# Query projection made directly in transposed form, with its token scale sent through DRAM, and a head order in the stacked tensors that keeps each transfer's destination in one piece

## The chip, the cores and the metric

The kernel runs on one core of one Trainium2 chip. The time is the device time of one execution in microseconds (us), and of several executions the median is given. TensorE (PE) does the matrix products, VectorE (DVE), ScalarE (ACT) and GpSimd (POOL) the elementwise work, and the sync engine (SP) issues nearly all DMA transfers of the part that the change touches.

## What is computed

A block with cross-attention and a mixture of experts. There are 32 batches of 112 tokens with 512 channels, 16 heads of 32 channels, and a context of 375 rows for each batch. The query projection is quantized: tokens and weight rows are rounded to integers with one scale each.

```python
def _w8a8_linear(x, w, b):
    qx, sx = _dyn_quant(x)            # integers, one scale a token
    qw, sw = _quant_weight(w)         # integers, one scale an output channel
    y = jnp.einsum('bnc,oc->bno', qx, qw) * (sx * sw[:, 0])
    return y + b
...
q = _w8a8_linear(x, wq, bq).reshape(B, N, H, D).transpose(0, 2, 1, 3)
k = (cond @ wk.T + bk).reshape(B, L, H, D).transpose(0, 2, 1, 3)
v = (cond @ wv.T + bv).reshape(B, L, H, D).transpose(0, 2, 1, 3)
scores = jnp.einsum('bhnd,bhld->bhnl', q, k) * inv_sqrt_d + mask[:, None]
attn = jax.nn.softmax(scores, axis=-1)
o = jnp.einsum('bhnl,bhld->bhnd', attn, v)
...
x = x + _L0_xattn_ref(_layernorm(x, axis=-1), ctx_2048, ...)
x = x + _L0_ffn_ref(_layernorm(x, axis=-1), ...)     # top 2 of 8 experts
```

## The kernel before

The program has four parts in a row: `prepare_weights` (to about 35 us of the trace), `attention` (to about 1115 us), `route` (to about 1160 us) and `experts` (the rest). Each part gives every engine a program of its own, and engines meet only at semaphores: `need(engine, semaphore, count)` lets an engine wait. Each engine takes its own instructions strictly in the order written.

`attention` is a software pipeline with one batch an iteration. Iteration `it` does the attention of batch `it` (stage a), the projections of batch n = it+1, the layer norm and rounding of the tokens of batch nn = it+2, the output projection of batch m = it-1 and the second layer norm and router of m2 = it-2. Inside an iteration all engines step through the heads h = 0 to 15. For each head PE turns the probabilities of two heads ago (line 563), makes the scores of head h (line 555), runs a share of the 28 projection steps (lines 591 and 596), and after certain heads a small piece of the other stages. The loop body covers two iterations and is passed 13 times; the first and the last iterations are written out.

The scores use a split of each float into two parts. For a head, the left operand `q_stack` holds 96 rows (q_hi, q_hi, q_lo of 32 channels each) and the right one `k_stack` holds k_hi, k_lo, k_hi. A projection comes out with 128 channels, that is 4 heads, on the partitions and groups of 4 heads side by side, so the stacked tensors are made by 36 small transfers from on-chip memory to on-chip memory in each iteration: 24 for keys (lines 276 to 280, 12 for each half of the heads) and 12 for queries (lines 313 to 317). Transfer i takes partitions 32 i to 32 i + 31, which hold the heads i, i+4, i+8, i+12. In `k_stack` and `q_stack` the heads stand in their natural order, so a destination is written in pieces four heads apart.

The query of batch n runs through these steps:
- h = 6: PE turns the rounded tokens `x_int` into `misc` (line 603), DVE copies them to `x_int_t` (494).
- h = 7: PE multiplies by `wq_int`, tokens on the partitions, four products of 512 columns (638).
- h = 8: DVE scales by the token's scale and by the row of weight scales into `q_tok` (498), POOL adds the bias row (357).
- h = 9: PE turns `q_tok` back, four transposes (603), and ACT makes `q_hi` from the result (424).
- h = 10: DVE makes `q_lo` (502). SP issues the 12 query transfers when it comes to them.

SP's order in one iteration is: 12 transfers of the second half of the keys of batch it, two weight loads (292, 293), the mask load (296), the stores of batch m2 (299, 301), the load of `x_res` (304), 12 transfers of the first half of the keys of batch n, 12 of its queries, the context and token loads (321, 323), and four weight stores (327, 328). The two key groups wait for the scores that still read the old keys (line 277's callers wait on `scored`). POOL's order is: the residual sum and the two small steps of the second norm, the sign of the mask (354), the query bias (357), the bias of `x_res` (361), the first norm's steps, the low part of the context (370) and of a piece of expert weights (375).

Of the kernel before, what the change touches and what calls it, by code (L numbers as in the profile page):

```python
# [4 lines left out]
F32 = mybir.dt.float32  # L5
# [3 lines left out]
ALU = mybir.AluOpType  # L9
# [3 lines left out]
H = 16  # L13
# [5 lines left out]
QUARTER = 32  # L19


def prepare_weights(nc, W, x, ctx_t, wq, wk_t, wv_t, wo, bq, bk, bv, bo, router_t):
# [6 lines left out]
    with ExitStack() as ctx:  # L29
# [10 lines left out]
        spread = sb("w_spread", [128, 2, KT, N])  # L40
# [9 lines left out]
        pairs = (("q", W["wq_int"], W["wq_row"]), ("o", W["wo_int"], W["wo_row"]))  # L50
# [5 lines left out]
        def _(sp):  # L56
# [5 lines left out]
            for dst, src in ((W["bq_row"], bq), (W["bv_row"], bv), (W["bo_row"], bo)):  # L62
                sp.dma_start(dst[:, :], src.rearrange("(a n) -> a n", a=1).to_broadcast([128, C])).then_inc(rows_loaded, 16)
            with nc.allow_non_contiguous_dma(reason="512 biases, once"):
                sp.dma_start(W["bk_col"][:, :], bk.rearrange("(g p) -> p g", p=128)).then_inc(rows_loaded, 16)
# [24 lines left out]
        def _(act):  # L90
# [15 lines left out]
            for i, (_, _, row) in enumerate(pairs):  # L106
                act.wait_ge(row_made, i + 1)
                act.activation(row[0:N, :], ps[0:N, :], ACT.Copy, scale=-inv_sqrt_d if i == 0 else 1.0).then_inc(row_out, 1)

        @block.vector  # L110
        def _(dve):
            for i, (n, _, _) in enumerate(pairs):
# [17 lines left out]
            for i, (_, dst, _) in enumerate(pairs):  # L130
# [6 lines left out]
            dve.tensor_scalar(W["bq_row"][:, :], W["bq_row"][:, :], -inv_sqrt_d, None, ALU.mult).then_inc(bias_done, 1)  # L137

        @block.tensor
        def _(pe):  # L140
            pe.wait_ge(ident_cast, 1)
            for i in range(2):
# [9 lines left out]
                pe.wait_ge(spread_done, KT * (i + 1))  # L152
                if i:
                    pe.wait_ge(row_out, i)
                for t in range(KT):
                    mm = pe.matmul(ps[0:N, 128 * t:128 * t + 128], spread[:, i, t, :], W["ident"][:, :],
                                   start=True, stop=True)
                mm.then_inc(row_made, 1)


def attention(nc, W, x, ctx_t, mask, x1, h2):
# [19 lines left out]
    with ExitStack() as ctx:  # L181
# [22 lines left out]
        q_tok = sb("q_tok", [N, C])  # L204
# [22 lines left out]
        q_made, q_out = sem("q_made"), sem("q_out")  # L227
        q_biased, q_hi_made, q_stacked = sem("q_biased"), sem("q_hi_made"), sem("q_stacked")
# [438 lines left out]
E = 8  # L667
# [512 lines left out]
```

## Time and profile before

| | |
|---|---|
| median of 3 runs | 1607.35 us (1606.39 to 1612.29) |
| profiled execution | 1609.71 us, its span from the first to the last instruction 1608.0 us |
| granted clock of TensorE, mean | 0.965 |
| busy: PE, DVE, ACT, POOL | 1494.6, 897.5, 884.0, 660.6 us |
| `attention` | about 35.8 to 1115 us |

A view of busy time tells how long each engine had an instruction under way. A timeline row gives start, duration, engine, line, operation and tiles. Matrix products overlap, so for PE the distance between two starts is the time that counts, and not the duration of one. "SPq" rows are SP's issue of a DMA: the duration is SP's own time, not the transfer's. What stands in brackets is idle time of the engine before the instruction, and what ended it.

### The profile page before, as it was taken

How to read it: one execution, taken by the hardware profiler on the slowest of the kernel's cores; microseconds unless marked ns; L12 is line 12 of the kernel's file. 1: busy time of each engine (PE TensorE's matmuls, PEld its weight loads, DVE VectorE, ACT ScalarE, POOL GpSimd, SP SyncE). 2: the span in 40 equal slices, each digit the busy share in tenths (PEclk: the TensorE clock that was granted, in tenths of full speed). 3: DMA queues.
4: the chain of work that ended last, by engine and by line, in shares of the span. 5: the costliest groups of instructions: out<-in, count | busy, mean ns of one | idle time of the engine just before them, and what ended most of it. 6: DMA issues, size and time to landing. Idle time of an engine off the chain costs nothing. (4 is left out here: it accounts for less than half of the span.)

```text
span 1608.0 us, 40123 instructions
## 1 busy us (share of the span) xinstructions
PE 1494.6 (93%) x11594; PEld 1317.6 (82%) x11595; DVE 897.5 (56%) x2365; ACT 884.0 (55%) x2097; POOL 660.6 (41%) x671
## 2 busy tenths in 40 slices
PE   2899999999999999999999999984399999999896
PEld 2788888888888888888888888873299999999895
DVE  6557666766676667666766676654632222222221
ACT  2467667677777776777677767761033333333232
POOL 4233334333443234323432343323555555656453
PEclk9999999999999999999999999985599999999998
DMA  5567777677767776777677767654537776666643
GB/s 173 145 170 196 209 200 197 179 228 205 194 178 226 202 196 179 225 205 196 178 225 201 200 179 222 185 142 141 160 68 186 182 175 134 148 154 125 160 77 48
DMA packets 220124, 281.09 MB, mean 175 GB/s; under 512 B 83568, under 2 KB 164976, under 8 KB 220080
## 3 DMA queue, kind: packets, MB, share of 16 engines
q1 hardware_dynamic: 203952, 247.24, 54.3%
q0 software_dynamic: 16128, 33.30, 11.6%
q8 instruction: 23, 0.38, 0.1%
q14 instruction: 21, 0.17, 0.0%
HBM read 118.31 MB, written 66.17 MB: 115 GB/s over the span
## 5 line engine op out<-in xcount | busy, mean ns | idle before, releaser
L464 DVE CUSTOM_DVE_ANT_0 probs<-score,neg_mask 112x375 f32<-112x375 f32 x512 | 279.7, 546 | 254.8 <-PE score L555 251.5
L392 ACT ACTIVATE probs<-probs,neg_max 112x375 f32<-112x375 f32 x512 | 312.3, 610 | 197.2 <-DVE neg_max L464 191.7
L563 PE MATMUL turn<-ident,probs 112*125 112x112 f32 x1536 | 264.8, 282 | 2.8 <-ACT probs L392 2.5
L385 ACT ACTIVATE probs_t<-turn 125x336 f32<-125x336 f32 x512 | 226.0, 441 | 71.6 <-PE turn L563 70.6
L563 PEld LDWEIGHTS turn<-ident,probs 112*125 112x125 f32 x1536 | 227.2, 190 | 36.4 <-issue 14.4
L555 PE MATMUL score<-k_stack,q_stack 96*112 96x376 f32 x512 | 209.4, 409 | 8.5 <-DMA q_stack<-q_lo 6.2
L591 PE MATMUL proj<-ctx_hi,wk_hi 128*128 128x376 f32 x512 | 176.0, 344 | 1.9 <-PEq L29 1.1
L591 PE MATMUL proj<-ctx_lo,wk_hi 128*128 128x376 f32 x512 | 172.0, 336 | 0.0
L591 PE MATMUL proj<-ctx_hi,wk_lo 128*128 128x376 f32 x512 | 171.7, 335 | 0.0
L1032 DVE TENSOR_TENSOR a_lo<-a_ps,a_hi 128x384 fp32r<-128x384 f32 x63 | 35.1, 557 | 243.7 <-ACT a_hi L1007 243.7
L596 PE MATMUL proj<-wv_hi,ctx_hi 128*125 128x512 f32 x384 | 151.8, 395 | 0.0
L596 PE MATMUL proj<-wv_hi,ctx_lo 128*125 128x512 f32 x384 | 151.7, 395 | 0.0
L596 PE MATMUL proj<-wv_lo,ctx_hi 128*125 128x512 f32 x384 | 151.0, 393 | 0.0
L354 POOL TENSOR_SCALAR neg_mask<-neg_mask 112x375 f32<-112x375 f32 x32 | 16.8, 525 | 305.2 <-DMA neg_mask<-mask 305.2
L370 POOL TENSOR_TENSOR ctx_lo<-ctx_stage,ctx_hi 128x1504 fp32r<-128x1504 f32 x31 | 106.6, 3437 | 57.9 <-ACT ctx_hi L429 57.9
L990 POOL DMA_INDIRECT out<-y_rows,scatter_idx x63 | 101.9, 1618 | 57.3 <-POOL scatter_idx L986 50.7
L375 POOL TENSOR_TENSOR w_raw<-w_raw,w_hi 128x1056 fp32r<-128x1056 f32 x32 | 78.9, 2467 | 92.9 <-ACT w_hi L434 92.9
L591 PEld LDWEIGHTS proj<-ctx_hi,wk_hi 128*128 128x128 f32 x512 | 97.4, 190 | 8.7 <-issue 1.5
L1020 ACT ACTIVATE y_rows<-y_ps,row_share 128x512 f32<-128x512 f32 x63 | 43.5, 691 | 106.7 <-PE y_ps L1102 73.3
L555 PEld LDWEIGHTS score<-k_stack,q_stack 96*112 96x112 f32 x512 | 92.4, 181 | 9.9 <-issue 7.5
L591 PEld LDWEIGHTS proj<-ctx_lo,wk_hi 128*128 128x128 f32 x512 | 97.6, 191 | 0.0
L591 PEld LDWEIGHTS proj<-ctx_hi,wk_lo 128*128 128x128 f32 x512 | 96.9, 189 | 0.0
(198 smaller groups left out, 3393.9 us busy)
## 6 DMA issues: line engine op xcount, KB each, us to landing
k_stack<-k_hi SPq DMA_DIRECT2D x512, 94.0 KB, 2.2
k_stack<-k_lo SPq DMA_DIRECT2D x256, 94.0 KB, 2.2
ctx_stage<-ctx_t SPq DMA_DIRECT2D x32, 750.0 KB, 5.0
q_stack<-q_hi SPq DMA_DIRECT2D x256, 56.0 KB, 2.0
w_raw<-gate_up_t SPq DMA_DIRECT2D x32, 352.0 KB, 3.1
gate_up_dram_hi<-w_hi SPq DMA_DIRECT2D x32, 352.0 KB, 4.8
gate_up_dram_lo<-w_raw SPq DMA_DIRECT2D x32, 352.0 KB, 5.2
gate_up_hi<-gate_up_dram_hi SPq DMA_DIRECT2D x16, 704.0 KB, 4.9
```

The source lines that it names most:

```text
L370: pool.tensor_tensor(c_lo[:, par % 2, :, :], stage[:, :, :], c_hi[:, par % 2, :, :].bitcast(F32), ALU.subtract).then_inc(c_lo_made, 1)
L375: pool.tensor_tensor(w_lo[:, :], w_raw[:, :], w_hi[:, :].bitcast(F32), ALU.subtract).then_inc(w_lo_made, 1)
L385: act.activation(probs_t[:, h % RING_T, :, :], turn[h % 2][0:LC, 0:LT * N].rearrange("p (l n) -> p l n", l=LT), ACT.Copy).then_inc(turned_ ...
L392: act.activation(probs[:, h % DS, :], probs[:, h % DS, :], ACT.Exp, bias=neg_max[:, par % 2, h:h + 1], scale=-1.0, accum_out=total[:, par ...
L464: dve.tensor_tensor_reduce(probs[:, h % DS, :], score[h % 2][0:N, 0:L], neg_mask[:, p, :], 1.0, BIG, ALU.add, ALU.min, neg_max[:, p, h:h + ...
L555: pe.matmul(score[h % 2][0:N, 0:LP], q_st[:, par % 2, h, :], k_st[:, h, :], start=True, stop=True).then_inc(scored, 1)
L563: mm = pe.transpose(turn[h % 2][0:LC, l * N:(l + 1) * N], probs[:, h % DS, l * LC:(l + 1) * LC], W["ident"][0:N, 0:N])
L591: mm = pe.matmul(bank[:, 0:LP], W[w][:, t, 128 * u:128 * u + 128], c[:, q, t, :], start=(t == 0 and w == "wk_hi" and c is c_hi), stop=(t = ...
L596: mm = pe.matmul(bank[0:LC, :], c[:, q, t, l * LC:(l + 1) * LC], W[w][:, t, :], start=(t == 0 and w == "wv_hi" and c is c_hi), stop=(t == ...
L990: pool.indirect_dma_start(out, bass.IndirectOffsetOnAxis(ap=si[par][:, 0:1], axis=0), y[:, par, :], None, compute_op=ALU.add).then_inc(sca ...
L1020: act.activation(y[:, other, :], y_ps[other][:, 0:C], ACT.Copy, scale=share[:, other:other + 1]).then_inc(y_made, 1)
L1032: dve.tensor_tensor(a_lo[:, :], a_ps[:, 0:FP], a_hi[:, :].bitcast(F32), ALU.subtract).then_inc(a_lo_made, 1)
```

## The change

The query projection is computed with output channels on the partitions, which is the layout that `q_hi` and `q_lo` need. PE uses `wq_int` as the left operand in 16 products of 128 channels by 112 tokens. The four transposes at h = 9 and their wait for POOL go. The weight scale and the bias then lie along the partitions (`wq_col`, `bq_col`), and the token scale lies along the free axis. `x_scale` is one number a partition, so it is stored to a small DRAM tensor `x_scales` by a new DMA at the end of SP's iteration it for batch nn, and read back one iteration later, repeated to all 128 partitions, by a second new DMA behind the store of `h_rows`. POOL multiplies it by `wq_col` into `q_scale` before the query bias. DVE scales `misc` by `q_scale` into `q_t` at h = 8, POOL adds the bias, ACT makes `q_hi` from `q_t` as soon as the bias is in, and DVE makes `q_lo` from `q_t`.

In `k_stack` and `q_stack` head h now stands at place h % 4 * 4 + h // 4. The heads that one transfer moves are then neighbours. PE picks the place by `stacked_at`.

In `prepare_weights` the row form of the query's weight scale is no longer made (4 products, 4 ACT copies and one eviction fewer). DVE executes 14 semaphore increments ahead of its first iteration (`LOOP_OFFSET`), which no one waits for.

```diff
@@ prepare_weights
-            for i in range(2):
-                act.wait_ge(scale_done, i + 1)
-                for t in range(KT):
-                    act.activation(spread[:, i, t, :], ones[:, :], ACT.Copy, scale=scale[:, i, t:t + 1]).then_inc(spread_done, 1)
+            act.wait_ge(scale_done, 2)
+            for t in range(KT):
+                act.activation(spread[:, t, :], ones[:, :], ACT.Copy, scale=scale[:, 1, t:t + 1]).then_inc(spread_done, 1)
...
+            dve.tensor_scalar(W["wq_col"][:, :], scale[:, 0, :], -inv_sqrt_d, None, ALU.mult).then_inc(bias_done, 1)
@@ attention, SP
-                        sp.dma_start(k_st[QUARTER * r:QUARTER * r + QUARTER, 8 * half + i:8 * half + 8:4, :].bitcast(F32),
+                        sp.dma_start(k_st[QUARTER * r:QUARTER * r + QUARTER, G4 * i + 2 * half:G4 * i + 2 * half + 2, :].bitcast(F32),
                                      src[rows, 2 * half:2 * half + 2, :].bitcast(F32)).then_inc(k_stacked[half], 16)
...
+                if has_n:
+                    need(sp, x_scale_stored, 16 * (n + 1))
+                    need(sp, q_scaled, n)
+                    sp.dma_start(x_scale_row[:, :], x_scales[n, :].rearrange("(a t) -> a t", a=1).to_broadcast([128, N])).then_inc(x_scale_in, 16)
...
-                            sp.dma_start(q_st[QUARTER * r:QUARTER * r + QUARTER, q, i:H:4, :].bitcast(F32),
+                            sp.dma_start(q_st[QUARTER * r:QUARTER * r + QUARTER, q, G4 * i:G4 * i + G4, :].bitcast(F32),
                                          src[rows, :, :].bitcast(F32)).then_inc(q_stacked, 16)
...
+                if has_nn:
+                    nn = it + 2
+                    need(sp, ln1, 8 * nn + 5)
+                    with nc.allow_non_contiguous_dma(reason="one scale a token"):
+                        sp.dma_start(x_scales[nn, :].rearrange("(p a) -> p a", a=1), x_scale[:, par % 2:par % 2 + 1]).then_inc(x_scale_stored, 16)
@@ attention, POOL
+                    need(pool, x_scale_in, 16 * (n + 1))
+                    need(pool, q_out, 3 * n)
+                    pool.tensor_tensor(q_scale[:, :, :], x_scale_row[:, :].unsqueeze(1).to_broadcast([128, G4, N]),
+                                       W["wq_col"][:, :].unsqueeze(2).to_broadcast([128, G4, N]), ALU.mult).then_inc(q_scaled, 1)
                     need(pool, q_out, 3 * n + 2)
-                    need(pool, q_made, 3 * n)
-                    pool.tensor_tensor(q_tok[:, :], q_tok[:, :], W["bq_row"][0:N, :], ALU.add).then_inc(q_biased, 1)
+                    pool.tensor_tensor(q_t[:, :, :], q_t[:, :, :], W["bq_col"][:, :].unsqueeze(2).to_broadcast([128, G4, N]),
+                                       ALU.add).then_inc(q_biased, 1)
@@ attention, ACT
                     if h == 9 and has_n:
-                        need(act, q_made, 3 * n + 3)
+                        need(act, q_biased, n + 1)
                         need(act, q_stacked, 16 * QDMAS * n)
-                        act.activation(q_hi[:, :, :], misc[:, 0:G4 * N].rearrange("p (g n) -> p g n", g=G4),
-                                       ACT.Identity).then_inc(q_hi_made, 1)
+                        act.activation(q_hi[:, :, :], q_t[:, :, :], ACT.Identity).then_inc(q_hi_made, 1)
@@ attention, DVE
                     if h == 8 and has_n:
-                        need(dve, q_made, 3 * n + 2)
-                        dve.scalar_tensor_tensor(q_tok[:, :], misc[0:N, :], x_scale[:, q:q + 1], W["wq_row"][0:N, :],
-                                                 ALU.mult, ALU.mult).then_inc(q_out, 1)
+                        need(dve, q_made, 2 * n + 2)
+                        need(dve, q_scaled, n + 1)
+                        dve.tensor_tensor(q_t[:, :, :], misc[:, 0:G4 * N].rearrange("p (g n) -> p g n", g=G4), q_scale[:, :, :],
+                                          ALU.mult).then_inc(q_out, 1)
...
+            for _ in range(LOOP_OFFSET):
+                waited(dve)
             iterations(dve, body)
@@ attention, PE
+            def stacked_at(h):
+
+                return h % 4 * G4 + h // 4
...
-                pe.matmul(score[h % 2][0:N, 0:LP], q_st[:, par % 2, h, :], k_st[:, h, :],
+                pe.matmul(score[h % 2][0:N, 0:LP], q_st[:, par % 2, stacked_at(h), :], k_st[:, stacked_at(h), :],
...
-                        for t in range(KT):
-                            mm = pe.matmul(misc[0:N, :], x_int_t[:, t, :], W["wq_int"][:, t, :], start=(t == 0), stop=(t == KT - 1))
+                        for g in range(G4):
+                            for t in range(KT):
+                                mm = pe.matmul(misc[:, g * N:(g + 1) * N], W["wq_int"][:, t, 128 * g:128 * g + 128], x_int_t[:, t, :],
+                                               start=(t == 0), stop=(t == KT - 1))
                         mm.then_inc(q_made, 1)
-                    if h == 9 and has_n:
-                        need(pe, q_biased, n + 1)
-                        turn_to_misc(lambda t: q_tok[:, 128 * t:128 * t + 128], W["ident"][0:N, 0:N], misc, N, 128).then_inc(q_made, 1)
```

On PE, at h = 7 and h = 9 of an iteration in the loop, before (`misc` is the shared result bank, `turn` the turned probabilities; "x4" is four instructions in a row):

```order
L638 MATMUL misc<-wq_int,x_int_t 112x512 x4
```

```order
L596 MATMUL proj<-wv_hi,ctx_hi 125x512
L596 MATMUL proj<-wv_lo,ctx_hi 125x512
L596 MATMUL proj<-wv_hi,ctx_lo 125x512
L603 MATMUL misc<-ident,q_tok 128x112 x4
L243 REGISTER_ALU
L563 MATMUL turn<-ident,probs 125x112 x3
```

The same two places after:

```order
L658 MATMUL misc<-x_int_t,wq_int 128x112 x16
```

```order
L615 MATMUL proj<-wv_hi,ctx_hi 125x512
L615 MATMUL proj<-wv_lo,ctx_hi 125x512
L615 MATMUL proj<-wv_hi,ctx_lo 125x512
L244 REGISTER_ALU
L582 MATMUL turn<-ident,probs 125x112 x3
```

The four wide products have become sixteen narrow ones, and behind the projection the turn of the probabilities follows at once.

On SP, from the second key group to the first, before (the mask load to the second of 12 key issues):

```order
L296 DMA neg_mask<-mask 112x375
L243 REGISTER_ALU
L299 DMA out<-y 112x512
L243 ISA
L301 DMA h_rows<-h_s 112x512
L243 REGISTER_ALU
L304 ISA
L304 DMA x_res<-x 112x512
L243 ISA
L243 REGISTER_ALU
L279 DMA k_stack<-k_hi 32x2x376
L279 DMA k_stack<-k_lo 32x2x376
```

And after:

```order
L297 DMA neg_mask<-mask 112x375
L244 REGISTER_ALU
L300 DMA out<-y 112x512
L244 ISA
L302 DMA h_rows<-h_s 112x512
L244 REGISTER_ALU
L306 DMA x_scale_row<-x_scales 128x112
L244 REGISTER_ALU
L309 ISA
L309 DMA x_res<-x 112x512
```

The fetch of the scale row has come in between the store of `h_rows` and the load of `x_res`.

SP at the turn from one iteration to the next, after (the last weight stores, the new store, the first key issues):

```order
L332 DMA gate_up_dram_lo<-w_raw 128x704
L333 DMA down_dram_lo<-w_raw 128x352
L244 ISA
L338 ISA
L338 DMA x_scales<-x_scale 112x1
L244 REGISTER_ALU x2
L280 DMA k_stack<-k_hi 32x752
L280 DMA k_stack<-k_lo 32x752
```

The new store stands between the weight stores and the second key group of the next iteration, and a key transfer is now written as 32 pieces of 752 numbers where it was 32 times 2 pieces of 376.

## Rows read from the trace of the kernel before

**Rows 1.** Windows: us, busy PE, PEld, DVE, ACT, POOL (instructions), clock, DMA share, GB/s.

```profile
400.00:600.00 200.00, 199.90 (x1719) 172.42 (x1718) 138.73 (x390) 142.77 (x355) 73.84 (x65) 1.00 0.72 201
```

**Rows 2.** Tile x_int_t, PE, 300 to 960 us: min/median/max ns, first and last start.

```profile
L638 PE MATMUL misc<-wq_int,x_int_t x84: 377/379/379, 303.5 to 949.4; 128*112 128x512 bf16 x84
```

**Rows 3.** Waits of PE, 50 to 232 us: us in total, times, longest.

```profile
PE score L555 <- DMA q_stack<-q_lo: 6.2, 4, 3.6
PE misc L603 <- POOL q_tok L357: 1.8, 2, 1.4
PE score L555 <- issue: 1.7, 2, 1.3
```

**Rows 4.** Waits of SP, 232 to 1000 us.

```profile
SPq L279 <- PE score L555: 11.9, 26, 1.1
SPq L327 <- POOL w_raw L375: 5.7, 18, 0.4
```

**Rows 5.** Timeline of PE in one iteration: start, us, then the instruction.

```profile
624.83 0.37 PE L603 MATMUL misc<-ident,x_int 112*128 112x112 bf16 x4
625.03 0.54 PE L563 MATMUL turn<-ident,probs 112*125 112x112 f32 x3
...
626.10 1.02 PE L638 MATMUL misc<-wq_int,x_int_t 128*112 128x512 bf16 x4
626.96 0.48 PE L563 MATMUL turn<-ident,probs 112*125 112x112 f32 x3
...
630.14 0.40 PE L596 MATMUL proj<-wv_hi,ctx_lo 128*125 128x512 f32 x1
630.49 0.60 PE L603 MATMUL misc<-ident,q_tok 112*128 112x112 f32 x4
630.93 0.49 PE L563 MATMUL turn<-ident,probs 112*125 112x112 f32 x3
```

**Rows 6.** Timeline of SP in the same iteration.

```profile
624.58 0.33 SPq L301 DMA_DIRECT2D h_rows<-h_s  x1
625.17 0.34 SPq L304 DMA_DIRECT2D x_res<-x  x1
...
632.36 0.60 SPq L279 DMA_DIRECT2D k_stack<-k_lo  x1
633.00 0.60 SPq L279 DMA_DIRECT2D k_stack<-k_hi  x1
```

**Rows 7.** Line 321: an issue with pieces on both sides, 128 partitions.

```profile
L321 SPq DMA_DIRECT2D ctx_stage<-ctx_t x31: 368/422/542, 35.8 to 996.6; - x31
```

**Rows 8.** DMA view, 300 to 900 us: KB each, median us to landing.

```profile
x_res<-x SPq DMA_DIRECT2D x19, 224.0 KB, 4.5
...
neg_mask<-mask SPq DMA_DIRECT2D x19, 164.1 KB, 3.4
```

**Rows 9.** Timeline of DVE and of POOL in the same iteration.

```profile
628.31 0.75 DVE L498 SCALAR_TENSOR_TENSOR q_tok<-misc,x_scale,wq_row 112x512 f32<-112x512 f32 x1
...
629.14 1.30 POOL L357 TENSOR_TENSOR q_tok<-q_tok,bq_row 112x512 f32<-112x512 f32 x1 [1.46 <-DVE q_tok L498]
```

**Rows 10.** Timeline around the first scores: SP, DVE, PE.

```profile
49.95 1.24 SPq L316 DMA_DIRECT2D q_stack<-q_hi  x2
...
49.19 0.62 DVE L502 TENSOR_TENSOR q_lo<-misc,q_hi 128x448 fp32r<-128x448 f32 x1 [0.22 <-ACT q_hi L424]
...
59.18 0.63 PE L555 MATMUL score<-k_stack,q_stack 96*112 96x376 f32 x1 [3.60 <-DMA q_stack<-q_lo]
```

**Rows 11.** Windows, the stretch behind the first score (columns as in Rows 1).

```profile
59.20:65.00 5.80, 5.80 (x20) 5.79 (x21) 1.67 (x6) 2.21 (x6) 0.00 (x0) 0.50 1.01 289
```

**Rows 12.** Timeline of PE in the preparation of the weights.

```profile
29.31 1.99 PE L156 MATMUL w_ps<-ident,w_spread 128*112 128x128 f32 x8
31.09 2.19 PE L149 MATMUL w_pt<-ident,w_ints 128*128 128x128 bf16 x16
```

**Rows 13.** DMA view, 240 to 1000 us, its only queue: packets, MB, share.

```profile
q1 hardware_dynamic: 134057, 151.98, 72.1%
```

More of the change, by code:

```diff
@@ L61, in _ @@
             sp.dma_start(W["x_in"][:, 0, :], x[0, :, :]).then_inc(W["x_in_ld"], 16)
-            for dst, src in ((W["bq_row"], bq), (W["bv_row"], bv), (W["bo_row"], bo)):
+            for dst, src in ((W["bv_row"], bv), (W["bo_row"], bo)):
                 sp.dma_start(dst[:, :], src.rearrange("(a n) -> a n", a=1).to_broadcast([128, C])).then_inc(rows_loaded, 16)
             with nc.allow_non_contiguous_dma(reason="512 biases, once"):
-                sp.dma_start(W["bk_col"][:, :], bk.rearrange("(g p) -> p g", p=128)).then_inc(rows_loaded, 16)
+                for dst, src in ((W["bk_col"], bk), (W["bq_col"], bq)):
+                    sp.dma_start(dst[:, :], src.rearrange("(g p) -> p g", p=128)).then_inc(rows_loaded, 16)
             sp.dma_start(W["router"][:, :, :], router_t.rearrange("(t p) e -> p t e", p=128)).then_inc(rows_loaded, 16)
@@ L104, in _ @@
             act.activation(W["c_hi"][:, 0, :, :], W["stage"][:, :, :], ACT.Identity).then_inc(W["c_hi_made"], 1)
-            for i, (_, _, row) in enumerate(pairs):
-                act.wait_ge(row_made, i + 1)
-                act.activation(row[0:N, :], ps[0:N, :], ACT.Copy, scale=-inv_sqrt_d if i == 0 else 1.0).then_inc(row_out, 1)
+            act.wait_ge(row_made, 1)
+            act.activation(W["wo_row"][0:N, :], ps[0:N, :], ACT.Copy).then_inc(row_out, 1)
         @block.vector
         def _(dve):
-            for i, (n, _, _) in enumerate(pairs):
+            for i, (n, _) in enumerate(pairs):
                 dve.wait_ge(loaded[n], 16)
@@ L128, in _ @@
                                       ALU.subtract).then_inc(ints_done, 1)
-            for i, (_, dst, _) in enumerate(pairs):
+            for i, (_, dst) in enumerate(pairs):
                 for t in range(KT):
@@ L151, in _, with attention @@
                     mm.then_inc(turned, 1)
-                pe.wait_ge(spread_done, KT * (i + 1))
-                if i:
-                    pe.wait_ge(row_out, i)
-                for t in range(KT):
[L156 to L161, printed above, removed]
+            pe.wait_ge(spread_done, KT)
+            for t in range(KT):
+                mm = pe.matmul(ps[0:N, 128 * t:128 * t + 128], spread[:, t, :], W["ident"][:, :],
+                               start=True, stop=True)
+            mm.then_inc(row_made, 1)
+def attention(nc, W, x, ctx_t, mask, x1, h2, x_scales):
     B, N, C = x.shape
@@ L203, in attention @@
         x_int, x_int_t = sb("x_int", [N, C], BF16), sb("x_int_t", [128, KT, N], BF16)
-        q_tok = sb("q_tok", [N, C])
+        q_t = sb("q_t", [128, G4, N])
+        x_scale_row, q_scale = sb("x_scale_row", [128, N]), sb("q_scale", [128, G4, N])
         out_ts = sb("out_ts", [128, G4, N])
@@ L636, in body @@
                         need(pe, q_out, 3 * n + 1)
-                        for t in range(KT):
-                            mm = pe.matmul(misc[0:N, :], x_int_t[:, t, :], W["wq_int"][:, t, :], start=(t == 0), stop=(t == KT - 1))
+                        for g in range(G4):
+                            for t in range(KT):
+                                mm = pe.matmul(misc[:, g * N:(g + 1) * N], W["wq_int"][:, t, 128 * g:128 * g + 128], x_int_t[:, t, :],
+                                               start=(t == 0), stop=(t == KT - 1))
                         mm.then_inc(q_made, 1)
-                    if h == 9 and has_n:
-                        need(pe, q_biased, n + 1)
-                        turn_to_misc(lambda t: q_tok[:, 128 * t:128 * t + 128], W["ident"][0:N, 0:N], misc, N, 128).then_inc(q_made, 1)
                     if h == 11 and has_m:
@@ L1127, in program @@
             W.update({n: sb(n, [128, 4, C], BF16) for n in ("wq_int", "wo_int")})
-            W.update({n: sb(n, [128, C]) for n in ("wq_row", "wo_row", "bq_row", "bv_row", "bo_row")})
-            W.update(bk_col=sb("bk_col", [128, 4]), router=sb("router", [128, 4, E]), minus_half=sb("minus_half", [128, 1]))
+            W.update({n: sb(n, [128, C]) for n in ("wo_row", "bv_row", "bo_row")})
+            W.update(bk_col=sb("bk_col", [128, 4]), bq_col=sb("bq_col", [128, 4]), wq_col=sb("wq_col", [128, 4]), router=sb("router", [128, 4, E]), minus_half=sb("minus_half", [128, 1]))
             LP = ctx_t.shape[2] + ctx_t.shape[2] % 2
```

19 lines of the change are left out of this document (10 added, 9 removed).

## The prediction

> **What bounds the kernel now.** I read the busy time by stretches first. From 400 to 600 us PE is busy for 199.90 of 200 us at the full granted clock, while DVE and ACT stand at about 70% [rows 1]. The page's slices show the same from about 230 to 1000 us. PE's waits say whether this is real: from 232 to 1000 us that view has no row at all, so nothing keeps PE waiting in the loop. The 84 records of the query product are 21 groups of four, from 303.5 to 949.4 us [rows 2], so an iteration takes 645.9 / 20 = 32.3 us, and all of it is PE's own work. Next I read SP, since it issues the 36 stacking transfers. In 768 us it waited 11.9 + 5.7 = 17.6 us [rows 4]. With 23.8 iterations in that stretch this is 0.74 us each, so SP works 31.5 of 32.3 us. It is the second bound, right behind PE. In the first iterations SP is even ahead of PE as a bound: from 50 to 232 us PE waits 6.2 us for `q_stack`, 1.7 us before other scores and 1.8 us for the biased `q_tok` [rows 3].
>
> **PE per iteration.** The four transposes of `q_tok` go. Before, the last projection product starts at 630.14, and the turn of the probabilities behind the transposes at 630.93 [rows 5], which is 0.79 us. Without them the turn follows one product later. A product of 512 columns takes (626.96 - 626.10) / 4 = 0.215 us in the quantized group [rows 5], and I take 0.23 for the projection. That saves 0.56 us, of which 0.12 was the wait for POOL (630.49 is 0.35 behind 630.14) and the rest the transposes.
> The query product had four matmuls in 0.86 us. The sixteen new ones have 112 columns in 16 bits, as the four transposes of `x_int` have, and these take 625.03 - 624.83 = 0.20 us, or 0.05 each [rows 5]. 16 x 0.05 = 0.80, which saves 0.06. Bounds: the narrow ones are only seen in fours, and if a row of sixteen were held up by its weight loads to the 0.11 us of the f32 transposes (0.44 us for four, rows 5), they would cost 1.76 us, a loss of 0.9. The nearest rows are the 16-bit ones, so I take 0.80. In sum 0.62 us an iteration, 31 times (the 32nd lies before the first score): 19 us.
>
> **SP per iteration, the condition for that.** SP gets two more issues. One costs 625.17 - 624.58 = 0.59 us with its register work [rows 6], so 1.2 us in all. With 0.74 us to spare and an iteration 0.6 us shorter, SP would be too slow if nothing else changed. The new head order is what can relieve it: the stacking issues cost 0.60 us each, one every 0.64 us, where issues with one piece for each partition cost 0.33 to 0.34 [rows 6]. The context load, in four pieces for each of 128 partitions, costs 0.42 [rows 7], so pieces alone don't explain 0.60. The rows don't tell whether the pieces, the 32 partitions or the way from on-chip memory to on-chip memory make the price. Bounds for the new issue are 0.34 and 0.60. I take 0.38, near the rows with one piece, so 36 x 0.22 = 8 us less. SP then works about 31.5 + 1.2 - 8 = 25 us and waits for others.
> What does SP's earlier coming collide with? Its key groups still wait for the scores that read the old keys, and its weight stores for POOL's low parts at the end of each iteration (both waits are there today, rows 4), so SP is held at two points of each iteration and can't run away. What becomes late next is nothing that PE needs.
>
> **The new waits.** POOL now stands in wait for the scale row, and behind it in POOL are the query bias, the bias of `x_res`, the norm's steps, and `ctx_lo`. DVE waits for `q_scale` at h = 8, and behind that are the score evictions of h = 9 and on. The fetch is issued behind the store of `h_rows`, at 624.58 before [rows 6]. SP starts its second key group at about 614, and with 12 issues cheaper by 0.22 each it comes to the fetch at about 622.5. Loads land in 3.4 us (mask) to 4.5 us (`x_res`) [rows 8], so the row is there at 626 to 627. POOL's product on 448 numbers a partition costs at most the 1.30 us of the 512 [rows 9], so `q_scale` is ready at 627.2 to 628.3, and DVE comes to its step at 628.31 [rows 9]. It is hidden, with little room. The round trip through DRAM is no limit: the store is issued some 9 us ahead of the fetch. DVE's own step gets cheaper (0.75 us, against 0.62 us for the like shape of `q_lo`, rows 9 and 10), POOL's total rises by 1.3 us on an engine that is busy for 74 of 200 us [rows 1], and ACT no longer waits for PE. All this lies beside PE's work and I cost it at nothing; without the cover a late row costs DVE up to 1 to 2 us an iteration, of which PE sees a part.
>
> **Ahead of the loop.** Preparation: the 8 records of line 156 at 29.31 go, and the transposes that start at 31.09 [rows 12] move forward by 1.8 us. ACT's last copy hangs on these, so the attention starts 1.8 us earlier. DVE's 14 increments cost at most some 0.7 us (a semaphore instruction at about 0.05 us, my estimate from the gaps between SP's issues) at a place where DVE has slack.
> First score: the query issues begin at 49.95 (right behind the keys) and the score starts at 59.18 after 3.60 us of idle PE [rows 10]. Twelve issues of 0.42 in place of 0.64 save 2.6 us, and without the transposes `q_lo` is ready about 0.5 us earlier: 3.1 us.
> Clock: behind this idle time the granted clock is 0.50 from 59.2 to 65 us [rows 11], that is 1.2 GHz in place of 2.4, and PE is busy all along. If the idle time shrinks to about half a microsecond, the clock should stay, and half of 5.8 us comes back: 2.9 us, bounds 0 and 2.9. I take all of it, since the drop came only after 3 us of idling.
> Early stalls: of rows 3, 6.2 - 3.6 = 2.6 us for later `q_stack`, 1.7 and 1.8, so 6.1 us, all caused by SP or by the removed wait. I take 6 us, bounds 2 and 6.1.
>
> **The sum.** 19 + 1.8 + 3.1 + 2.9 + 6 = 33 us. Against the profiled execution of 1609.7 us this gives 1576.7. Its time lies 2.4 us above the median of the runs, so I forecast 1574 us.
>
> **Rivals.** (1) The stacking issue stays at 0.60 us, because its price is in the on-chip to on-chip transfer and not in the pieces. For it speaks that keys (2 pieces) and queries (4 pieces) both cost 0.60, against it the 0.42 of the context load. Then SP bounds: 31.5 + 1.2 = 32.7 us against 32.3 now, so 0.4 x 27 = 11 us, and 1.2 us more in each of the four early iterations that SP already bounds, 5 us, less 1.8 from the preparation: +14, about 1621 us. SP decides from an issue of about 0.57 us upward, since it must save 32.7 - 31.7 = 1 us over 36 issues.
> (2) The scale row is late in most iterations. POOL waits, DVE waits behind it, the evictions of h = 9 and 10 slip by 1 to 2 us, and PE sees part of it at the turn of the probabilities two heads later. At 0.5 us an iteration the gain falls by 15: 1589 us. Against it: the row has a microsecond or so to spare, and POOL and DVE wait today too.
> (3) Only the loop gains: SP's early lateness and the clock's drop stay. 19 + 1.8 = 21 us: 1586 us.
> (4) Code loading. In the loop the DMA view shows only data packets [rows 13], so no engine loads code again in a pass. The change shifts and lengthens every engine's loop. If one of them, say DVE's, no longer stays loaded, each of the 13 passes waits for a load, which in this trace lands in 3.4 to 4.5 us [rows 8]; with some 2 us of it hidden by DVE's idle time, 13 x 2 = 26 us: 1600 us.
> The Trainium skill's page "Runtime: NRT & Kernel Launch", section "Instruction fetch mechanics", says that a taken branch whose target isn't in the current window of two pages makes the engine wait for a fetch. The trace of before agrees in that its loop, which stays loaded, shows no such packets; which side the new code falls on no row here can show.
>
> **How the numbers follow.** The forecast gets 68%, rival 1 8%, rival 2 9%, rival 3 10%, rival 4 5%. The forecast's own range is 1568 (if the transposes' share is 0.7 us and all else comes true) to 1582. To leave no more than 2 in 10 out it must reach rivals 2 and 3: 1566 to 1592. A measurement here can tell about 0.5%, or 8 us: below 1599.3 is faster, above 1615.4 slower. The forecast and rivals 2 and 3 give 87% faster, rival 4 mostly no change (6% with the edge of others), rival 1 slower (7%).
>
> **What would show it.** Right: the loop's period falls from 32.3 to about 31.7 us with PE still without waits; the stacking issues take 0.34 to 0.4 us; SP's waits rise to some 7 us an iteration; no transposes of q; the first score near 54 us; no stretch at clock 0.5 behind it; sixteen products in 0.8 us. Wrong: SP still issuing at 0.60, with PE waiting for `k_stack` or `q_stack` in the loop; DVE idle before `q_t`, with POOL as the cause; instruction packets between 240 and 1000 us; sixteen products that take well over 0.9 us.

## The result: 4.7% slower

| | before | after |
|---|---|---|
| median of 4 runs | 1607.7 us (1606.4 to 1612.3) | 1680.6 us (1676.4 to 1694.1) |
| ratio | | 1.0474, 95% interval 1.0447 to 1.0501 (the two medians alone: 1.0453) |
| span of the profiled execution | 1608.0 us | 1674.7 us |
| granted clock, mean | 0.965 | 0.965 |
| busy: PE, DVE, ACT, POOL | 1494.6, 897.5, 884.0, 660.6 us | 1495.6, 894.2, 865.8, 689.0 us |

PE has as much to do as before and takes 67 us longer, so it waits. The window of [rows 1] shows it in the changed kernel, at the same clock (us, busy PE, PEld, DVE, ACT, POOL, clock, DMA share, GB/s):

```profile
400.00:600.00 200.00, 189.97 (x1675) 163.93 (x1674) 129.42 (x369) 132.36 (x337) 72.05 (x63) 1.00 0.73 191
```

The query product gives the period, as in [rows 2]; the 304 records are 19 groups of sixteen. The last record starts 0.75 us behind the first one of its group, so an iteration takes (939.9 - 0.75 - 320.4) / 18 = 34.38 us. By the same reckoning, with 0.65 us for a group of four, it took (949.4 - 0.65 - 303.5) / 20 = 32.26 us before.

```profile
L658 PE MATMUL misc<-x_int_t,wq_int x304: 212/213/223, 320.4 to 939.9; 128*128 128x112 bf16 x152
```

The waits from 232 to 1000 us (us in total, times, longest), where PE had no row before, and SP those of [rows 4]:

```profile
DVE q_t L512 <- POOL q_scale L367: 80.0, 22, 5.0
...
POOL q_scale L367 <- DMA x_scale_row<-x_scales: 33.2, 22, 2.4
...
PE misc L622 <- DVE o_int L462: 23.7, 21, 1.2
...
PE turn L582 <- ACT probs L406: 12.5, 32, 1.5
...
PE score L574 <- DMA k_stack<-k_hi: 6.6, 5, 3.0
```

```profile
SPq L293 <- DMA down_dram_lo<-w_raw: 20.0, 11, 3.7
SPq L321 <- DVE q_lo L516: 13.7, 18, 1.8
SPq L280 <- PE score L574: 5.0, 10, 0.6
```

In every iteration DVE stands 3.6 us for `q_scale`, and PE then waits for DVE's and ACT's results; sometimes it waits for keys. SP has a wait that it never had: for the weights that it stored to have landed. Its waits sum to 38.7 us in 22.3 iterations, 1.7 us each, so it works about 32.6 of the 34.4 us, and stands still for the rest. One iteration in the timeline:

```profile
628.63 0.96 PE L658 MATMUL misc<-x_int_t,wq_int 128*128 128x112 bf16 x16
...
629.10 0.37 SPq L306 DMA_DIRECT2D x_scale_row<-x_scales  x1
...
633.27 0.53 POOL L364 TENSOR_SCALAR neg_mask<-neg_mask 112x375 f32<-112x375 f32 x1 [12.88 <-DMA neg_mask<-mask]
...
634.62 0.93 POOL L367 TENSOR_TENSOR q_scale<-x_scale_row,wq_col 128x448 f32<-128x448 f32 x1 [0.83 <-DMA x_scale_row<-x_scales]
```

```profile
635.66 0.62 DVE L512 TENSOR_TENSOR q_t<-misc,q_scale 128x448 f32<-128x448 f32 x1 [4.57 <-POOL q_scale L367]
```

The fetch is issued 0.47 us after PE began the product that its row is to scale. POOL takes its instructions in order, so ahead of `q_scale` it also waits for the mask, which SP issues 1.7 us before the fetch (627.40): 11.9 us an iteration, and 8.9 before. So the row is late, and so is the mask. And the stacking issues are as long as before; the first line below is SP's issue of a key transfer, the second that of the new store (min/median/max ns):

```profile
L280 SPq DMA_DIRECT2D k_stack<-k_hi x355: 512/591/912, 241.5 to 999.9; - x178
```

```profile
L338 SPq DMA_DIRECT2D x_scales<-x_scale x23: 332/508/1578, 239.7 to 996.8; - x23
```

### The profile page after: what moved, and what is told of

Same layout as the page of the kernel before. It is cut to its first block and busy times, and to the rows that moved or that the text cites. A ratio compares the mean times of both kernels' runs of the same rounds, so it can differ in the third digit from the quotient of the medians.

```text
span 1674.7 us, 40904 instructions
## 1 busy us (share of the span) xinstructions
PE 1495.6 (89%) x11842; PEld 1317.3 (79%) x11843; DVE 894.2 (53%) x2366; ACT 865.8 (52%) x2092; POOL 689.0 (41%) x703
## 5 line engine op out<-in xcount | busy, mean ns | idle before, releaser
L582 PE MATMUL turn<-ident,probs 112*125 112x112 f32 x1536 | 268.8, 284 | 22.4 <-ACT probs L406 21.8
```

Of the source, the lines that this page charges most:

```text
L582: mm = pe.transpose(turn[h % 2][0:LC, l * N:(l + 1) * N], probs[:, h % DS, l * LC:(l + 1) * LC], W["ident"][0:N, 0:N])
```

## The experiments

Two theories stood at the start. S: SP's own time sets the period, since the head order saved nothing and two transfers came on top. W: the late row stops POOL, DVE and PE. A third one, L, came with the runs: the small store lands slowly and makes the landings of other transfers late. Each "before" below is the median of the kernel before, measured on the same chip beside the run. What is added to or taken from the changed kernel is set against its 1680.6 us, which had a before of 1607.7.

**The head order alone**, in the kernel before:

```diff
-  k_st[QUARTER * r:QUARTER * r + QUARTER, 8 * half + i:8 * half + 8:4, :]
+  k_st[QUARTER * r:QUARTER * r + QUARTER, G4 * i + 2 * half:G4 * i + 2 * half + 2, :]
   (and so for q_st, read at stacked_at(h))
```

> The kernel before with the new head order in k_stack and q_stack and nothing else. The prediction's step on the head order said that the stacking issue falls from 0.60 to about 0.38 us; PE bounds the loop before, so the gain would be only in the early iterations, some 6 to 9 us: about 1600 us. The reading of the changed kernel says that the issue stays at 0.59 us whatever the pieces: no change, 1607 us within 3, and stacking issues still 0.59 to 0.60 us.

1604.9 us against 1606.8, ratio 1.0003 (0.9982 to 1.0023): no change. The order did merge the pieces, since the queue's packets from 240 to 1000 us fell from the 134057 of [rows 13] to 88772. But the issue is the same to 0.01 us (585/597/1552 ns before at this line), and SP's waits from 232 to 1000 us rose only from 17.6 to 30.8 us: the order frees some 0.5 us of SP an iteration, not 8:

```profile
L279 SPq DMA_DIRECT2D k_stack<-k_hi x381: 507/591/928, 234.0 to 999.2; - x191
```

**The two transfers alone**, in the kernel before. The store stands behind the weight stores and the fetch behind the store of `h_rows`, as in the change; nothing reads the row.

> The kernel before with the two new transfers added to SP at the places of the change, and nothing that reads the fetched row. Theory S (SP's own time sets the period): SP works 31.5 us of 32.3 before, and two issues with their register work add 1.2 us or, where the store's issue is as long as its 1.1 to 1.6 us in the changed kernel, up to 2.2 us, so the period becomes 32.7 to 33.7 us and the time 1620 to 1645 us. Theory W (the late scale row stops POOL, DVE and then PE, and SP alone is still covered): at most 1612 us.

1677.9 us against 1606.8: +71 us, nearly the whole loss, with the old query. It lies above the ranges of both theories, of S (1620 to 1645) and of W (at most 1612).

**The changed kernel with a constant row in place of the fetched one** (it leaves the tokens' scale out of the query):

```diff
+  x_row_unused = sb("x_row_unused", [128, N])          # the fetch goes here
-  need(pool, x_scale_in, 16 * (n + 1))
+  pool.memset(x_scale_row[:, :], 0.01)                 # once, ahead of the iterations
```

> The changed kernel with both transfers still made, but the fetch goes to a tile that no one reads and POOL multiplies a constant row, set once: the token scale is left out of the query and nothing waits for the transfer. Theory S: SP has the same work, so the time stays within some 10 us of the changed kernel, 1670 to 1681 us, and PE waits for stacked keys or queries. Theory W: the 3.66 us an iteration that DVE stood before q_t go, and what is left is SP's bound of the first rival or PE's: 1590 to 1625 us.

1666.2 us: the wait for the row is worth 1680.6 - 1666.2 = 14 us, and 59 us stay without it. This lies in neither theory's range. The row's lateness is the smaller part. DVE still waits for `q_scale` (from 232 to 1000 us), 2.3 us an iteration and not 3.6, because POOL still waits for the mask ahead of it:

```profile
DVE q_t L514 <- POOL q_scale L367: 51.1, 22, 3.9
```

**The same without both transfers**:

> As the run without the wait, and without both transfers: the query is made transposed, its token scale is left out, and SP has the instructions of the kernel before. Both theories expect PE's gain of 0.6 us an iteration to show, down to SP's own 31.5 us: 1580 to 1592 us. A third theory, that the transposed form itself costs (sixteen products, or the shorter way from one product group to the next), expects over 1610 us.

1593.8 us against 1606.8, ratio 0.9929 (0.9910 to 0.9949), some 2 us over the range. So the change without its transfers does gain, and the two transfers cost 1666.2 - 1593.8 = 72 us. Windows and the product's row (320 records, 20 groups, 31.74 us an iteration) of this kernel:

```profile
400.00:600.00 200.00, 199.95 (x1785) 174.21 (x1783) 142.63 (x405) 143.52 (x358) 79.11 (x68) 1.00 0.71 200
```

```profile
L651 PE MATMUL misc<-x_int_t,wq_int x320: 212/213/225, 327.7 to 931.5; 128*128 128x112 bf16 x160
```

**Store and fetch apart**, each alone in the kernel before:

> The kernel before with the store of the token scales added at its place behind the weight stores, and no fetch. With both transfers the same kernel took 1677.9 us, 71 us over before, and the store takes 1.2 to 1.3 us of SP's time an iteration there against 0.65 us for the fetch. SP is 0.5 to 0.7 us short of being the bound before. If the loss is SP's time alone: 31.5 + 1.25 = 32.75 against 32.3, so 0.45 to 0.9 us an iteration and some 5 us in the early ones: 1620 to 1640 us. If the small store's landing is what costs (it makes the weights' buffers or the next keys late), it stays nearer to both together: above 1650 us.

> The kernel before with one more load at the place of the fetch, of the same shape (112 numbers repeated to 128 partitions, into a tile that no one reads) but from the tokens, so that it waits for no store. SP's time alone: 31.5 + 0.65 = 32.15, still under PE's 32.3, so hardly a loss: 1607 to 1615 us. If the repeated row costs the queues more than SP's issue shows: above 1625 us.

The store gave 1653.5 us (+46), the fetch 1623.8 us (+17, in neither range). Both are more than SP's issue was reckoned to cost. With the fetch alone the issue behind it is longer: `x_res` was 338 ns and is 799 ns. This isn't so with the store beside it: there the median of `x_res` is 348 ns in the kernel before and 342 in the changed one. So the longer issue can be part of the 17 us, but not of the changed kernel's loss.

```profile
L308 SPq DMA_DIRECT2D x_res<-x x19: 453/799/1304, 304.6 to 894.6; - x19
```

**Both transfers moved to ScalarE**:

```diff
+  if h == 1 and has_n:   act.dma_start(x_scales[n, :]..., x_scale[...])      # waits for ln1
+  if h == 4 and has_n:   act.dma_start(x_scale_row[:, :], x_scales[n, :]...) # waits for the store's landing
```

> The changed kernel with both transfers issued by ScalarE instead of SP: the store behind head 1 and the fetch behind head 4 of the iteration in which the row is used. The result is the full one. Theory S (SP's own time made the loss, and the late row followed from it): about as the run without either transfer, 1588 to 1600 us, with SP at its time of before and DVE hardly waiting for q_scale. If the transfers themselves hurt, through the shared DMA queues or the wait of POOL and DVE for the row, the loss stays in good part: above 1625 us.

1734.8 us (+128), worse than on SP. The timeline of ScalarE tells why: the store is issued at 648.70, its fetch can go only at 658.94. PE then waits for ScalarE's copy of `h_t`, 2.9 us an iteration, and the granted clock from 400 to 600 us is 0.93, where it was 1.00.

```profile
648.70 0.35 ACTq L425 DMA_DIRECT2D x_scales<-x_scale  x1
...
658.94 0.37 ACTq L430 DMA_DIRECT2D x_scale_row<-x_scales  x1
659.43 0.54 ACT L433 ACTIVATE h_t<-misc 128x448 f32<-128x448 f32 x1 [4.26 <-DMA x_scales<-x_scale]
```

```profile
PE misc L646 <- ACT h_t L433: 58.1, 20, 5.2
```

448 bytes had landed only after some 10 us, where the stores of 224 KB (`out`) land in 3.6 us in the kernel before. Theory S doesn't explain this; it led to theory L.

**The store alone, on ScalarE**, waited for an iteration later:

```diff
+  if h == 15 and has_n:   need(act, x_scale_stored, 16 * (n + 1))
+  if h == 15 and has_nn:  act.dma_start(x_scales[nn, :]..., x_scale[...])
```

> The kernel before with the store of the token scales alone, issued by ScalarE behind its last head (an issue there took 0.35 us), and waited for only an iteration later. The same store on SP cost 46 us, more than the 1.33 us of SP's time an iteration explains beside 0.5 to 0.7 us of slack (some 25 us). If SP's time, with the hold-up of its issue behind the four weight stores, is all of it: no loss here, 1604 to 1614 us. If the slow landing of the small store (8 to 12 us where it was waited for) makes the other transfers late in the shared queues: still 20 us or more over before, above 1625 us.

1672.2 us (+65): SP issues not one transfer more than before, and the loss is larger than with the store on SP. So most of the store's cost isn't its issue on SP. SP's waits from 232 to 1000 us show where it goes:

```profile
SPq L293 <- DMA down_dram_lo<-w_raw: 37.8, 21, 3.2
```

In each iteration SP stands 1.8 us until the weight stores have landed, which took 5.4 us before (`down_dram_lo`, median) and held up nothing.

**Both on ScalarE, the fetch later**:

> The changed kernel with both transfers on ScalarE, the store behind its last head and the fetch behind head 5, some 12 us later, so that ScalarE need not stand in wait for the store's landing as it did in the run before (75.7 us in 20 iterations). If that wait was the whole loss of the other version: 1590 to 1605 us, under the kernel before. If the row, fetched behind head 5 and landing 5.5 us later, comes too late for the product at head 8: DVE waits again for q_scale and the time is 1610 to 1640 us.

1666.9 us (+59), above both ranges. ScalarE's wait was not the whole loss. Nor does the row come late here: POOL waits for it once, for 0.7 us. But SP waits for the weights' landing here too (43.1 us in 22 iterations), and POOL for the mask 12.7 us an iteration (8.9 before), so `q_scale` is late all the same and DVE waits 46.2 us for it.

**What is slow in the store.** It stays on SP, alone in the kernel before, with 512 bytes a partition, or with the same 4 bytes a partition set apart:

```diff
-  x_scales (B, N)         <- x_scale[:, par % 2:par % 2 + 1]
+  x_scales (B, N, 128)    <- ident[0:N, :]                          # storewide
+  x_scales (B, N, 128)[:, :, 0:1]  <- x_scale[...]                  # storespread; 16 and 64 in the last two
```

> The kernel before with a store on SP at the place of the new one, of 512 bytes from each of 112 partitions (rows of the identity, into a scratch tensor) instead of 4. If any store at this place costs what the small one does, through SP's time: 1645 to 1660 us. If the 4-byte writes are what is slow: SP's bare issue of some 0.6 us is left, as with the fetch: 1608 to 1622 us.

> The kernel before with the small store of 4 bytes from each of 112 partitions, each number 512 bytes behind the last one in memory instead of side by side. If writes of 4 bytes are slow in themselves, or through their number: as the store side by side, 1645 to 1660 us. If it is that 112 writes fall into the same few hundred bytes: near the wide store, under 1625 us.

> The kernel before with the small store, its 4-byte writes 64 bytes apart. Side by side it took 1653.5 us, 512 bytes apart 1618.0. If the loss comes from writes that fall into one short stretch of a few tens of bytes: near 1618 us. If it needs a distance of several hundred bytes: 1635 to 1655 us.

> As the run before, 256 bytes apart. Under both theories no slower than at 64 bytes; if what the writes share is a stretch of 512 bytes, two fall into one and a part of the loss stays: 1622 to 1640 us; otherwise 1618 us within 4.

1617.9 us (+11) for 512 bytes a partition, and 1618.0 (+11), 1617.9 (+13) and 1618.5 (+13) for 4 bytes that lie 512, 256 and 64 bytes apart, against 1653.5 (+46) side by side. So 35 us of the store's 46 are there only when the 112 writes of 4 bytes lie side by side; their size or number alone doesn't make them. The DMA view from 300 to 900 us shows it in the landings of others (KB each, median us). The store side by side:

```profile
w_raw<-gate_up_t SPq DMA_DIRECT2D x18, 352.0 KB, 3.7
...
neg_mask<-mask SPq DMA_DIRECT2D x18, 164.1 KB, 4.3
x_scales<-x_scale SPq DMA_DIRECT2D x18, 0.4 KB
```

512 bytes apart:

```profile
w_raw<-gate_up_t SPq DMA_DIRECT2D x19, 352.0 KB, 3.1
...
neg_mask<-mask SPq DMA_DIRECT2D x19, 164.1 KB, 3.5
x_scales<-x_scale SPq DMA_DIRECT2D x18, 0.4 KB, 5.2
```

Apart, the mask lands in 3.5 us as in [rows 8] (3.4), and the store itself in 5.2. The queue (packets, MB and the share of the 16 engines' time, 260 to 1000 us) shows that it is the DMA engines that are held: side by side they are busy for longer with fewer bytes. The first line is with the store side by side, the second 512 bytes apart:

```profile
q1 hardware_dynamic: 127527, 142.40, 75.6%
```

```profile
q1 hardware_dynamic: 132128, 148.38, 73.2%
```

Counted in the same traces over the whole span, the packets that took more than 1 us are 746 with the store side by side, half of them (379) key transfers' packets of 1504 bytes, and 183 with the store apart. They are 170 in the kernel before and 808 in the changed one. This bears out theory L. Why such writes hold the engines the runs don't show, and the changed kernel itself was not run with its store set apart.

That a store on ScalarE's queue delays landings on SP's is what the Trainium skill's page "DMA: Bandwidth & Descriptors" lets one expect, in its section on queues, rings and completion order: the write that reports a transfer's end lands only after all earlier writes of the same DMA engine, across its queues. The trace agrees: the mask's landing rose from 3.4 to 4.3 us with the store on the other queue. The same page's specifications say that transfers under 512 bytes are done by reading, changing and writing back. By this alone the 4-byte writes would be as slow 512 bytes apart as side by side; measured are 1618.0 and 1653.5 us, so that rule alone doesn't account for the loss.

**The 14 increments** ahead of DVE's first iteration, taken away, or 7 in their place:

```diff
-  LOOP_OFFSET = 14
+  LOOP_OFFSET = 0        # offset0; 7 in offset7
```

> The changed kernel without the 14 increments that DVE executes ahead of its first iteration. Theories S and W both expect nothing: 1676 to 1686 us. The fourth rival (code of one engine's loop is loaded again in each pass) would see a shift of 14 instructions as a change of some 20 us in either direction and as instruction packets between 260 and 1060 us.

> The changed kernel with 7 increments ahead of DVE's first iteration in place of 14. Without any it took 1788.8 us, with DVE idle twice a pass for 6.3 and 6.6 us and five instruction packets a pass. If 14 are only just enough, 7 show the same packets and 1700 to 1790 us. If any shift of some instructions is enough: 1676 to 1686 us, with no such packets.

1788.8 us and 1820.4 us, 108 and 140 us over the changed kernel, where some 20 had been expected of the first and the second lies above its range. Both theories were wrong here, and the fourth rival's mechanism is real. In DVE's timeline without increments, at the turn of an iteration:

```profile
636.17 0.55 DVE L477 CUSTOM_DVE_ANT_0 probs<-score,neg_mask 112x375 f32<-112x375 f32 x1 [6.57 <-issue]
...
643.65 0.55 DVE L477 CUSTOM_DVE_ANT_0 probs<-score,neg_mask 112x375 f32<-112x375 f32 x1 [6.26 <-issue]
```

and in its DMA view from 260 to 1000 us, where the changed kernel has only the data queue (45 packets with 7 increments):

```profile
q14 instruction: 46, 0.38, 0.2%
```

DVE waits for nothing that the profile shows, twice a pass, and such packets are there in number only in the kernels with these stops (at most 2 in the others). With 14 increments there are none, so code loading has no part in the change's loss. Why 7 are worse than none can be read in part from the waits (232 to 1000 us; no increments first, then 7). DVE stands still about as long in sum, but once a pass and not twice, for 13.6 us each and not 7.1, and PE waits longer behind it. What places the stops stays open.

```profile
DVE probs L477 <- issue: 141.7, 20, 9.8
...
PE turn L582 <- ACT probs L406: 96.0, 29, 6.7
```

```profile
DVE probs L477 <- issue: 149.4, 11, 18.1
...
PE turn L582 <- ACT probs L406: 143.6, 21, 17.5
```

Part of the price is TensorE's clock: from 400 to 600 us it was granted at 0.91 and 0.87, and at 1.00 with 14 increments.

**Without the way through DRAM.** PE makes the row at h = 6 in columns of `turn0` that the turned probabilities leave free, ScalarE copies it, and the rest is as in the change:

```diff
+  pe.matmul(turn[0][:, LT * N:LT * N + N], x_scale[:, q:q + 1].to_broadcast([N, 128]), W["ident"][0:N, 0:N], start=True, stop=True)
+  act.activation(x_scale_row[:, :], turn[0][:, LT * N:LT * N + N], ACT.Copy)
-  (the store and the fetch)
```

> The changed kernel without the way through DRAM: PE makes the row of token scales by one product of the scales, repeated over 128 columns, with the identity, into free columns of a turn bank, ScalarE copies it, and POOL multiplies it as in the change. The result is the full one. SP has the instructions of the kernel before. The run without either transfer gave 1593.8 us; the product adds 0.11 us an iteration on PE, the copy some 0.3 us on ScalarE: 1592 to 1600 us, 0.5 to 1% under the kernel before. If the row by way of PE, ScalarE and POOL is late at head 8, DVE waits for q_scale and the gain is gone: 1605 us or more.

1596.1 us against 1607.6, ratio 0.9931 (0.9917 to 0.9945): 0.7% faster than the kernel before, clear of the noise, and 84 us faster than the changed one. Only 161 packets take over 1 us here. The first line is PE's product for the row; the next instruction starts at 615.00, so it costs PE 0.30 us where 0.11 had been expected. DVE hardly ever waits for `q_scale` (from 232 to 1000 us). The 323 records are the last three of a group and twenty whole groups, so the period is (937.2 - 299.8) / 20 = 31.87 us, 0.13 above that without any row:

```profile
614.70 0.46 PE L634 MATMUL turn<-ident,x_scale 112*128 112x112 f32 x2
```

```profile
DVE q_t L510 <- POOL q_scale L358: 1.3, 3, 0.8
```

```profile
L662 PE MATMUL misc<-x_int_t,wq_int x323: 212/213/224, 299.8 to 937.2; 128*128 128x112 bf16 x162
```

## Why the prediction was wrong

The forecast was 1574 us in a range of 1566 to 1592; it became 1680.6. By the medians the way there is: the change without its two transfers -13, the two transfers +72, the wait for the row +14.

- **The bounds** were read rightly: PE first, SP 0.7 us behind it. What followed from it, that SP decides, was seen and then argued away.
- **The step that failed first is the stacking issue** of 0.38 us in place of 0.60, 8 us an iteration. It stayed at 0.59 in every kernel with the new order. The three explanations named (pieces, 32 partitions, on-chip memory to on-chip memory) were left open and the value was taken near the row that promised most. The pieces are now out; which of the other two makes the price no run tells. With it the first rival's condition held: SP has no time to spare.
- **The first rival's price** of 1621 us was too low by 60 us, and not for SP's own work: its 31.5 + 1.2 = 32.7 us an iteration is what SP works in the changed kernel (32.6). What the prediction had at nothing is what the store does to other transfers. Side by side it costs 35 us more than the same store set apart, with SP waiting for landings that held up nothing before. The prediction looked at the store's round trip only as a question of when the row is back ("no limit"), and had no row of a transfer with 4-byte pieces. Another 6 of the 72 us were lost before the first score, as told below. If the 35 us carry over from the kernel before, some 30 are left; how they divide between SP's two issues, the fetch and their meeting with the store no run tells.
- **The new waits, costed at nothing**, cost 14 us for the row alone, the size of the second rival (15). The cover was worked out with the cheaper issues: SP was to reach the fetch at 622.5, which is 3.6 us ahead of the product's start at 626.10. It reached it 0.47 us behind that start. The cover also left out that POOL must get past the mask first; 2.3 of DVE's 3.6 us stayed when nothing waited for the row.
- **PE's part** was right. The sixteen products take 0.80 us as predicted (the turn behind 628.63 starts at 629.43). At h = 9 without the transfers the turn follows the last projection product by 0.23 us (624.98 to 625.21), 0.79 before, so the 0.56 came too. But the loop gained 32.26 - 31.74 = 0.52 us, not 0.62: averaged over 20 iterations, the turns and scores stand 0.08 us further apart than before, for which no run gives the cause.
- **Ahead of the loop** the terms of 13.8 us were mostly wrong. Without the transfers SP's first load goes 1.6 us earlier (34.23 against 35.83), near the 1.8, but the first key issue only 0.3 us (41.32 against 41.63). The first score came at 58.81 us in place of 59.18, not near 54, since twelve issues still take 7.6 us. The early stalls didn't go either: from 50 to 232 us PE's waits sum to 9.6 us, and to 10.3 before. The granted clock behind the first score stayed at 1.00, so the clock's term came in this run, but not because of the idle time alone. That fell from 3.60 to 1.68 us; in the kernel without the way through DRAM it was 1.81 and the clock of the same stretch 0.71, and with the head order alone 3.37 and again 0.71. In the changed kernel the first score was even later, by 5.8 us: with no iteration between store and fetch yet, SP issued the store at 40.28 and the fetch, which waits for its landing, only at 47.09, with the keys behind it, and DVE stood for the row. With the constant row it is still 65.08 against 58.81, so 6 us are the transfers' own.

```profile
58.81 0.40 PE L567 MATMUL score<-k_stack,q_stack 96*112 96x376 f32 x1 [1.68 <-DMA q_stack<-q_lo]
```

```profile
59.20:65.00 5.80, 5.80 (x39) 5.67 (x38) 3.07 (x10) 4.40 (x12) 0.00 (x0) 1.00 1.01 301
```

```profile
52.02 0.62 DVE L512 TENSOR_TENSOR q_t<-misc,q_scale 128x448 f32<-128x448 f32 x1 [6.01 <-POOL q_scale L367]
...
64.97 0.63 PE L574 MATMUL score<-k_stack,q_stack 96*112 96x376 f32 x1 [4.34 <-DMA q_stack<-q_lo]
```

(The first two fences are of the kernel without transfers, the last one is of the changed kernel.)

- **The fourth rival** (code loading) didn't happen, but only thanks to the increments, and its price of 2 us a pass was mis-sized: 108 us over 13 passes are 8.3 us each. The prediction had costed the increments at 0.7 us and not asked what they do. It cited the Trainium skill's page "Runtime: NRT & Kernel Launch", section "Instruction fetch mechanics", by which a taken branch to code outside the current window makes the engine wait for a fetch. The trace without increments agrees: 46 instruction packets, and DVE still for 7.1 us twice a pass.

## What to carry to other kernels

Where the engine that issues transfers is a second bound, cost every added transfer at its issue and at what its landing does to the others, and let no sum rest on a cheaper issue that no row shows: two transfers of 56 KB together cost more here than all that the edit could gain. A column of single numbers stored side by side to DRAM was such a transfer; where numbers had to go from partitions into a row, one small matrix product with the identity did it here for 2 us in 1600. And when the length of a loop's code changes, look for instruction packets in the loop first, since here 14 instructions ahead of it decided over 108 us.

## What was not expected of the hardware

- 112 writes of 4 bytes side by side in DRAM cost 46 us over 32 iterations, 64 bytes or more apart 11 to 13; the one was waited for some 10 us, the other landed in 5.2 (512 bytes apart). Packets that took over 1 us, nearly all of them of other transfers, rose from 170 to 746.
- A small store on one queue delays the landing of transfers on the other: the mask 3.4 to 4.3 us, SP's wait for stored weights 0 to 1.8 us an iteration.
- The issue of a transfer from 32 partitions to 32 others takes SP 0.59 to 0.60 us whether it has 4, 2 or 1 pieces a partition.
- Behind a load of 112 numbers repeated to 128 partitions the next issue took 799 ns in place of 338, but 342 to 348 ns where the small store ran too; no run tells why.
- With 0 or 7 instructions ahead of DVE's loop the kernel takes 108 and 140 us more than with 14.
